# A linear-attention layer in front of a convolution layer: the group norm applied to the turned x on ScalarE, and VectorE's small operations in another order

## What is computed

```python
def _gn(v, G=32, eps=1e-5):            # per image and group of 4 channels
    ...
    return ((g - m) / jnp.sqrt(s + eps)).reshape(v.shape)

# layer 0, on _gn(x): linear attention, 4 heads of 32
q, k, v = split(x @ w_qkv)
q = softmax(q, axis=-2) * scale        # over the 32 numbers of a head
k = softmax(k, axis=-1)                # over the 16384 positions
context = einsum('bhdn,bhen->bhde', k, v)
out = einsum('bhde,bhdn->bhen', context, q) @ w_out + b_out
return layer_norm(out) * g_ln + b_ln
```

## Time and profile before

| | |
|---|---|
| median of 3 runs | 6668.7 us (6665.32 to 6675.22) |
| the profiled execution | 6692.88 us, its span 6691.1 us |
| mean granted clock of TensorE | 0.953 of full speed |
| busy share of the span | PE 86%, DVE 68%, POOL 62%, ACT 54% |

### The profile page before, as it was taken

One profiled execution on the slowest core, in us unless ns is written; L12 is line 12 of the kernel. 1 busy time (PEld: TensorE's weight loads), 2 busy tenths in 40 slices (PEclk: granted clock), 3 DMA queues, 4 the chain that ended last, 5 costly groups with the idle time before them and its releaser, 6 DMA issues. The chain is left out here.

```text
span 6691.1 us, 144257 instructions
## 1 busy us (share of the span) xinstructions
PE 5749.4 (86%) x51796; PEld 5262.7 (79%) x51796; DVE 4552.6 (68%) x5284; ACT 3640.7 (54%) x4872; POOL 4150.8 (62%) x3608
## 2 busy tenths in 40 slices
PE   6789999999999999999995368888888888888887
PEld 5678888888888888888884368788888888787887
DVE  6367777777777777777773786676776666666653
ACT  5555555555555555555541445555555555555554
POOL 0146666666666666666667687677776777676651
PEclk8899999999999999999998689999999999999999
DMA  5356676666766667666656469999999999999987
GB/s 129 125 156 207 201 219 200 206 201 206 214 204 202 200 204 214 204 202 201 198 169 174 130 170 252 251 261 262 263 266 256 255 266 258 255 259 252 262 246 216
DMA packets 1239334, 1441.35 MB, mean 215 GB/s; under 512 B 142960, under 2 KB 1025396, under 8 KB 1238516
## 3 DMA queue, kind: packets, MB, share of 16 engines
q1 hardware_dynamic: 1238516, 1431.07, 75.5%
HBM read 999.09 MB, written 431.64 MB: 214 GB/s over the span
## 5 line engine op out<-in xcount | busy, mean ns | idle before, releaser
L1257 PE MATMUL psC<-wide,xhl 128*128 128x256 bf16 x6144 | 1052.5, 282 | 57.9 <-DMA wide<-toeplitz_wide 40.7
L1254 PE MATMUL psC<-wide,xhl 128*128 128x192 bf16 x6144 | 873.3, 252 | 0.0
L1187 POOL TENSOR_TENSOR stage<-stage,nrow 128x1024 f32<-128x1024 f32 x240 | 612.0, 2550 | 387.5 <-DMA stage<-x_by_block_row 377.8
L1204 POOL COPY down<-xhl 48x448 f32<-48x448 f32 x512 | 516.0, 1008 | 491.7 <-PE psC L1263 387.5
L813 POOL TENSOR_TENSOR y<-y,grow 128x1024 f32<-128x1024 f32 x256 | 603.6, 2358 | 323.7 <-DVE y L657 323.7
L1348 ACT ACTIVATE xhl<-psC 128x512 f32<-128x512 f32 x512 | 303.6, 599 | 694.7 <-PE psC L1263 693.1
L824 POOL TENSOR_TENSOR q<-q,qinv 128x1024 f32<-128x1024 f32 x256 | 489.9, 1914 | 307.4 <-DVE qinv L731 307.4
L1263 PE MATMUL psC<-narrow,down 128*128 128x96 bf16 x6144 | 536.4, 212 | 164.6 <-POOL down L1207 95.2
L657 DVE TENSOR_TENSOR y<-psProj,rstd 128x1024 f32<-128x1024 f32 x256 | 313.6, 1225 | 515.6 <-POOL rstd L805 515.6
L1455 DVE SCALAR_TENSOR_TENSOR xhl<-xhl,psC 128x512 f32<-128x512 f32 x512 | 346.9, 680 | 465.9 <-ACT xhl L1348 465.7
L1254 PEld LDWEIGHTS psC<-wide,xhl 128*128 128x128 bf16 x6144 | 644.6, 116 | 17.6
(11 more groups left out here) (181 smaller groups left out, 14591.1 us busy)
## 6 DMA issues: line engine op xcount, KB each, us to landing
wide<-toeplitz_wide SPq DMA_DIRECT2D x1024, 140.0 KB, 5.9
xa<-in_x SPq DMA_DIRECT2D x256, 512.0 KB, 4.7
xb<-in_x SPq DMA_DIRECT2D x256, 512.0 KB, 3.8
xc<-in_x SPq DMA_DIRECT2D x256, 512.0 KB, 5.7
x_rows<-xc SPq DMA_DIRECT2D x256, 512.0 KB
res<-x_rows SPq DMA_DIRECT2D x256, 512.0 KB, 9.0
out<-res SPq DMA_DIRECT2D x256, 512.0 KB, 8.0
stage<-x_by_block_row SPq DMA_DIRECT2D x225, 512.0 KB, 9.0
```

Of the source, the lines that this page charges most:

```text
L1187: nc.gpsimd.tensor_tensor(v, v, nrow[:, 0:1, :].to_broadcast([P, NP_, C]), ALU.mult).then_inc(s_scaled, 1)
L1204: nc.gpsimd.tensor_copy(dst[lo, :, :, 0:last], src[lo, :, 0:NQ, CW:])
L1254: nc.tensor.matmul(dst[:, :, :, 2:], lhs, tab[:, :, 32 + part * 12:44 + part * 12], start=False, stop=False)
L1257: nc.tensor.matmul(dst, lhs, tab[:, :, part * 16:part * 16 + 16], start=(n == 0), stop=False)
```

## The change

- `wqk`, `shb`, `tq`, `bk`, `ones` and everything that fills them are gone: no scaled weights, no shift matmul (L565), no `split_bias`, no bias matmuls (L514). Keys and queries use `wqkv`.
- ACT normalises `xT[n]` in place: `Identity` with scale and shift from `norm`. Chunk 0 at step 0, behind the copy of `ek` and once `s_norm` is there; each other chunk one step ahead, behind `corr`. PE's `keys` waits for `x_normed`.
- The square of the statistics is now taken from `xT[n-1]` in SBUF, in the next step between the exponential of q and that of k; that of the last chunk follows its copy at once.
- `add_up` of a chunk moves to the next step, right behind `row_sums`; only the last chunk's stays at step 0 before `mean_context`.
- At step 0 `norm_weights` stands ahead of `scale_rows`.
- Small DVE operations on one column (`ksum`, `nmax`, `var`, the shift) become `tensor_scalar` with pointer scalars.

The core of the diff:

```diff
             def keys(img, n, ga, gb):
-                if n == 0:
-                    pe.wait_ge(s_wk, img + 2)
+                pe.wait_ge(x_normed, gb + 1)
                 pe.wait_ge(qt_taken, upto(gb - 1))
                 pe.wait_ge(q_subbed, upto(gb))
-                pe.wait_ge(t_taken, gb + 1)
...
-                for hf in range(2):
-                    nc.tensor.matmul(out[:, hf * 512:(hf + 1) * 512].rearrange("p (t d) -> p t d", d=P),
-                                     ones[:], bk[:].to_broadcast([BK, 4, P]), start=True, stop=False)
-                    for t in range(4 * hf, 4 * hf + 4):
-                        mm = nc.tensor.matmul(out[:, t * P:(t + 1) * P], xT[n][:, t * P:(t + 1) * P],
-                                              wqk[:, 0:C], start=False, stop=(t % 4 == 3))
+                for t in range(TPC):
+                    mm = nc.tensor.matmul(out[:, t * P:(t + 1) * P], xT[n][:, t * P:(t + 1) * P],
+                                          wqkv[:, 0:C], start=True, stop=True)
...
         def _(act):
+            def normalise(n, gb):
+                nc.scalar.activation(xT[n][:], xT[n][:], ACT.Identity, bias=norm[:, 1:2], scale=norm[:, 0:1]
+                                     ).then_inc(x_normed, 1)
+
+            def square(n, count):
+                act.wait_ge(t_taken, count)
+                return nc.scalar.activation(junk[:], xT[n][:], ACT.Square, accum_out=part_sums[:, 1, n:n + 1])
...
+                    if n == 0 and image_live(img + 1):
+                        act.wait_ge(s_norm, img + 2)
+                        act.wait_ge(t_taken, gb + 1)
+                        normalise(n, gb)
+                    if live(img, gb - 1):
                         act.wait_ge(q_subbed, gb)
                         v = q[(n - 1) % 2]
                         nc.scalar.activation(v[:], v[:], ACT.Exp).then_inc(s_qexp, 1)
+                    if live(img, ga - 1) and n:
+                        square(n - 1, ga)
...
+                    if n + 1 < steps and image_live(img + 1):
+                        act.wait_ge(t_taken, gb + 2)
+                        normalise(n + 1, gb + 1)
...
-                        nc.scalar.activation(junk[:], src, ACT.Square, accum_out=part_sums[:, 1, n:n + 1])
-                        nc.scalar.activation(xT[n][:], src, ACT.Identity, accum_out=part_sums[:, 0, n:n + 1]
+                        nc.scalar.activation(xT[n][:], psR[n % 2][:], ACT.Identity, accum_out=part_sums[:, 0, n:n + 1]
                                              ).then_inc(t_taken, 1)
+                        if n == NCH - 1:
+                            square(n, ga + 1).then_inc(s_sq0, 1)
...
-                nc.vector.scalar_tensor_tensor(ksum[:, m + 1:m + 2], ksum[:, m:m + 1], corr[:, m:m + 1],
-                                               ksum_c[:, m:m + 1], ALU.mult, ALU.add)
+                nc.vector.tensor_scalar(ksum[:, m + 1:m + 2], ksum[:, m:m + 1], corr[:, m:m + 1],
+                                        ksum_c[:, m:m + 1], ALU.mult, ALU.add)
...
-                nc.vector.tensor_tensor(nmax[:, n + 1:n + 2], nmax[:, n:n + 1], nmax_c[:, n:n + 1],
-                                        ALU.min).then_inc(s_nmax, 1)
+                nc.vector.tensor_scalar(nmax[:, n + 1:n + 2], nmax_c[:, n:n + 1], nmax[:, n:n + 1], None, ALU.min
+                                        ).then_inc(s_nmax, 1)
...
                     if live(img, gc - 2):
                         row_sums(img, n, gc)
+                    if live(img, gb - 2) and n != 1:
+                        add_up((n - 2) % NCH, gb - 1)
...
+                    if n == 0 and image_live(img + 1):
+                        norm_weights(img, gb)
                     if live(img, gc - 2):
                         scale_rows(n, gc)
...
-                    if n == 0 and image_live(img + 1):
-                        norm_weights(img, gb)
                     if n == 0 and live(img, gb - 1):
-                        add_up(n, gb)
+                        add_up(NCH - 1, gb)
+                    if n == 0 and live(img, gb - 1):
                         mean_context(img, gb)
-                    if n == 0 and image_live(img + 1):
-                        split_bias(img)
                     if live(img, gb):
                         max_k(n, gb)
                     if live(img, gb - 1):
                         sum_q(n, gb)
-                        if n:
-                            add_up(n, gb)
```

More of the change, by code:

```diff
@@ L329, in layer0 @@
         s_pow = sem("b_stat_pow")
[L330 to L334, removed]
+        s_norm = sem("b_norm_ready")
+        x_normed = sem("b_xT_normed")
         k_ready = sem("b_keys")
@@ L362, in layer0 @@
         s_x1 = sem("b_x1")
+        s_sq0 = sem("b_last_squared")
         g_done = sem("b_gram")
@@ L447, in _ @@
             pe.wait_ge(s_const, 16 * NCONST)
-            pe.wait_ge(s_chain, 14)
+            pe.wait_ge(s_chain, 13)
             def buffer(n, turn):
@@ L496, in keys @@
             def keys(img, n, ga, gb):
-                if n == 0:
-                    pe.wait_ge(s_wk, img + 2)
+                pe.wait_ge(x_normed, gb + 1)
                 pe.wait_ge(qt_taken, upto(gb - 1))
                 pe.wait_ge(q_subbed, upto(gb))
-                pe.wait_ge(t_taken, gb + 1)
                 out = buffer(n, 2)
                 for hf in range(2):
-                    mm = nc.tensor.matmul(out[:, hf * 512:(hf + 1) * 512], wqk[:, C:2 * C],
+                    mm = nc.tensor.matmul(out[:, hf * 512:(hf + 1) * 512], wqkv[:, C:2 * C],
                                           xT[n][:, hf * 512:(hf + 1) * 512], start=True, stop=True)
@@ L561, in image @@
                     if live(img, gb):
[L562 to L566, removed]
                         keys(img, n, ga, gb)
@@ L633, in _ @@
             t = Tally(dve, s_chain)
-            t.then(nc.vector.memset(ones[:], 1.0 / 32))
             t.then(nc.vector.memset(acc[:], 0.0))
@@ L658, in scale_rows, with reduce_sums @@
                                         ).then_inc(s_y, 1)
-            def reduce_sums(gb):
+            def reduce_sums(img, gb):
                 dve.wait_ge(t_taken, gb + NCH)
+                dve.wait_ge(s_sq0, img + 2)
                 nc.vector.tensor_reduce(sums1[:], part_sums[:], AX.X, ALU.add).then_inc(s_red, 1)
             def norm_weights(img, gb):
-                base = (img + 1) * 5
+                base = (img + 1) * 4
                 dve.wait_ge(s_stat, img + 2)
@@ L668, in norm_weights @@
                 dve.wait_ge(s_st, base + 1)
-                nc.vector.tensor_tensor(var[:], stat[:, 0:1], stat[:, 0:1], ALU.mult).then_inc(s_st, 1)
+                nc.vector.tensor_scalar(var[:], stat[:, 0:1], stat[:, 0:1], -1.0, ALU.mult, ALU.mult).then_inc(s_st, 1)
                 dve.wait_ge(s_st, base + 2)
-                nc.vector.tensor_tensor(var[:], stat[:, 1:2], var[:], ALU.subtract).then_inc(s_st, 1)
+                nc.vector.tensor_scalar(var[:], var[:], stat[:, 1:2], None, ALU.add).then_inc(s_st, 1)
                 dve.wait_ge(s_st, base + 3)
@@ L674, in norm_weights @@
                 dve.wait_ge(s_pow, img + 2)
[L675 to L704, removed]
-                nc.vector.scalar_tensor_tensor(ksum[:, m + 1:m + 2], ksum[:, m:m + 1], corr[:, m:m + 1],
-                                               ksum_c[:, m:m + 1], ALU.mult, ALU.add)
+                nc.vector.tensor_scalar(norm[:, 1:2], stat[:, 0:1], norm[:, 0:1], -1.0, ALU.mult, ALU.mult
+                                        ).then_inc(s_norm, 1)
@@ L707, in add_up @@
+            def add_up(m, count):
+                dve.wait_ge(ctx_done, count)
+                dve.wait_ge(s_corr, count)
+                dve.wait_ge(acc_done, upto(count - 1))
+                nc.vector.tensor_scalar(ksum[:, m + 1:m + 2], ksum[:, m:m + 1], corr[:, m:m + 1],
+                                        ksum_c[:, m:m + 1], ALU.mult, ALU.add)
                 nc.vector.scalar_tensor_tensor(acc[:], acc[:], corr[:, m:m + 1], psC[:, 0:C],
```

15 lines of the change are left out of this document (3 added, 12 removed).

## The result

The changed kernel takes 6468.3 us, the median of 4 runs (6448.5 to 6477.8), against 6671.4 us for the kernel before: a ratio of 0.9693, 95% interval 0.9668 to 0.9717, 203 us less. The prediction said 205 us less (6464). The profiled execution took 6477.8 us with a span of 6476.0.

What follows compares the result with a forecast made beforehand. PE's work and a ring through DVE were taken as bounds, POOL's ring close behind. 7.8 + 4.0 + 1.4 = 13.2 us an image, 198 in 15, plus 7 for the image before: 205 less, 6464 us; range 6445 to 6485 (0.57).

Steps and rivals of the forecast that it cites:

- The inner step: One chunk step inside an image: from 12.20 to 11.6 us, 0.60 gained in each of 13 intervals, 7.8 an image.
- no wait, but no room either: Before `turn_q` in the inner step: `centre_q` ends 2.7 us behind `project`'s start, `turn_q` could begin at 2.7 to 2.8.
- `add_up` and the minimum: DVE in the inner step: `add_up` (1.09 us) moves into a wait of 2.04; the minimum goes from 0.41 to 0.2.
- The first rival: Small DVE operations stay held by POOL, costing at chunks 0, 1 and 2: 56 us, 6520 in all; chance 0.22.
- The bias matmuls: Two matmuls ahead of the query matmuls on PE: without them 0.44 us less work, PE alone 11.58 us a step.
- two rings of nearly one length: Inner step: PE's own work, 12.0 us, and the ring from keys through DVE's operations and `turn_q` back to keys.
- The slower rival: Normalisation on ScalarE, ahead of `sqo`, becomes the ring: at 5.5 us a piece 56 us slower, 6725; chance 0.02.
- The ring through POOL: `project`, `sqo`, POOL's `q`, `turn_q`: at least 11.5 us; as rival two steps last 23.1 + 0.5, 6503; chance 0.15.
- The end of an image: Boundary from chunk 15 to chunk 0: keys follow context without a wait; sum 3.7 us, taken as 4.0 an image.
- The example of the kernel before: The one image end read for the forecast, B = 1627.17: its step ends at B+22.6, forecast B+18.9.
- more gain: Rival at image ends: PE may keep its full clock, 1.7 us an image, 26 us, 6438; chance 0.04.
- the stop of 3.43 us: Behind the end of chunk 15's `centre_q`: a stop that nothing in the profile releases, forecast to stay.

Runs made afterwards that it cites:

- halved gram: Changed kernel with half of `gram_of` (8 of its 16 matmuls) ahead of `turn_q`: 6400.2 us, ratio 0.9584.
- second power: Changed kernel with a second power on GpSimd in every step, into a spare tile, ahead of `rstd`: 6673.7 us, ratio 0.9989.
- padded kernel: Changed kernel with one more one-column memset on DVE in every step, behind `add_up`: 6467.4 us, ratio 0.9675.
- keys made to wait: Changed kernel with the keys of chunk 0 also waiting for the image's mean context: 6488.4 us, ratio 0.9707.

## Why the prediction was right, point by point

*The total.* That 203 and 205 us lie so close is in part luck. By the traces the first layer became 217 us shorter (the last `centre_q` ends at 3283.1 instead of 3500.4), 12 more than forecast: the ends of images gave more than their terms and the inner steps less. The profiled execution of the kernel before lay 21.5 us above its median and that of the changed kernel 9.5, and this difference takes the 12 us away again.

*The inner step.* Forecast 11.6, measured 11.68. That PE's work would bound it is nearly right: with the bias matmuls back it is 12.12, so each part of a microsecond on PE counts. What I had called "no wait, but no room either" costs 0.15 us or more: `centre_q` can't begin before the queries end (DVE waits 0.58 us for them), and `turn_q` follows its end, so the bound is a ring through PE and DVE of 11.68 us. The halved gram removes it (11.49). The gain was 0.50 us a step where 0.60 was forecast.

*`add_up` and the minimum.* Cost 0 in the new places, as forecast. The trace before could not tell the place from the form. The runs do: undone alone, the place costs 6 us and the form 34, both together 100. The unheld forms take 0.27 (`ksum`) and 0.21 us (`nmax`), near the 0.2 I took; both are covered.

*The first rival* (the small operations stay held) fell. The one-column `tensor_scalar` runs beside POOL, and so does a one-column copy. The Trainium skill, "VectorE: DVE Perf Modes", section "What auto-detection actually checks", gives the two-port mode by the "outermost non-unit dims". The prediction read this as covering a column copied to a column, which has no such dimension beside the partitions; the measurement decides that it isn't covered. For the two-column copy, 1.74 us, the trace agrees with the rule. The price of the rival was put at 56 us. The old forms cost 34 by the medians and 48 in the trace; in 15-0 it is 1.2 us instead of 2.1, as I had given L689's hold in full.

*The bias matmuls.* 0.44 us forecast and measured (12.12 against 11.68). Alone, without DVE's edits, they give 0.22: that two rings of nearly one length must both be shortened was the step of the argument on which the size hung.

*ScalarE.* The normalisation was put at 1.1 us and takes 1.23, the square fits with 0.23 us to spare. The slower rival's room was right: 2.46 us more on ACT make the step 12.0, as its formula gives with 3 x 1.23 us, (23.1 + 0.9) / 2, and the kernel is not slower than before. Its account lacked `ctxg`, which stands behind the normalisation at chunk 0.

*The ring through POOL.* Put at 11.5 us a step and never last. The prediction's first sum for it, 14.18 + 0.1 - 2.82, reads like a ring of one step, by which the second power would have made the step 13.1 us or more. The 12.29 measured shows that it returns over two steps, as the 23.1 us in the rivals have it.

*The end of an image.* Forecast 4.0, measured 6.1; this term was mis-sized. From the keys' start to the end of the step the sum holds: B+11.65 to 18.9 forecast, 7.25 us, and 8.88 to 16.13 measured, also 7.25. What came earlier was context, at B+7.0 to 9.4 instead of 9.85. Most of the 2.1 us beyond the forecast are TensorE's clock, at two places:

- Behind the wait before the keys. The example of the kernel before, 22.6 us, was one of its two shortest image ends in the loop; the mean is 23.54. At nine of the eleven the granted clock fell to half between B+13.8 and B+15.4, about where PE ended its wait for `acc` (2.4 to 4.4 us at the eleven), and work behind it ran slower than in the earlier trace rows, where the keys took 1.94 us. The end 208 us behind the example shows it:

```profile
1849.50 0.71 PE L565 MATMUL psCtx<-wqkv,shb 128*96 128x128 f32 x2 [2.93 <-DVE acc L707]
1850.01 3.19 PE L504 MATMUL psR<-xT,wqk 128*128 128x512 f32 x4
```

In the changed kernel this wait is gone, and the clock doesn't fall there at any end. The mean lies 0.9 us above the example, of which the forecast had allowed 0.3 (for the hold on L722).

- Behind PE's stop at the branch. Gram in the example of the kernel before ran at half clock, 3.38 us from 1631.21 on, and nine of the eleven ends were like it; in the changed kernel six are. At those six the step takes 18.4 us on average, near the 18.9 forecast, at the other five 16.4: 0.9 us in the mean.

In the stretch from 590 to 2900 us of the two traces the granted clock is at half for 75 us before and 20 after. So this was the rival "more gain", with a chance of 0.04 and 26 us (1.7 an image). It came true, and the smaller gain in the inner steps made up for a part of it. Why the clock falls at one end and not at another isn't shown. At the branch it isn't DVE's stop, as the padded kernel too has 20 us. The length of PE's own stop there goes with it only loosely: it is 1.6 to 2.3 us in the changed kernel, 2.3 to 3.0 before and 2.3 to 2.7 with the bias matmuls back, where ten of eleven ends fall; but it also fell behind 1.92 us and not behind 2.30 in one trace. In front of the keys and at chunk 0 to 1 the rows are clearer: nine of eleven ends fell behind waits of 2.4 to 4.4 us (before) and of 2.09 us (old forms), none behind 1.14 us (the keys made to wait) or 0.78 us (the changed kernel).

*The reason given for that term was partly wrong.* I had let the new place of `norm_weights` free the shift of POOL's hold of 2.30 us. The form alone does it: in the old place the shift takes 0.21 us beside POOL's `y`, and the time is the same. And that the stop of 3.43 us stays was wrong; put back by padding it cost 0.3 us an image end.

## What to carry to other kernels

Where two rings are of nearly one length, price an edit by what the second leaves, and look for the edit on the other ring that pays only together with it. An operation held by another engine's has two cures, another place or another form; one is enough, and the form keeps its worth where the schedule slips. Once one engine's own work is the bound, look at its last small wait: other work that is ready, put ahead of the waiting instruction, gave here 68 us for a few moved matmuls. And where a stretch varies from one repetition to the next, read several: the one image end that the forecast went by was 0.9 us shorter than their mean.

## What was unexpected of the hardware

- A one-column copy or `tensor_scalar` between SBUF tensors runs beside a GpSimd `tensor_tensor` (0.15 to 0.27 us), while a two-column copy waits for its end (1.74 us), and so do one-column operations with two SBUF tensors (up to 2.30 us).
- The length of an engine's program in a loop matters: with 16 one-column memsets more per image (191 operations instead of 175) DVE stops for 3.0 to 3.3 us behind the branch, without them it waits 0.36, and that for ScalarE.
- Reading and writing 1024 columns of SBUF in place with scale and bias takes ScalarE 1.23 us, against 1.05 for a square out of SBUF and 1.03 out of PSUM.
- TensorE's granted clock at the image ends was at half (1.2 of 2.4 GHz) for 75 us of 2300 before and for 20 after. Behind PE's stop at the branch very similar rows go either way: 1.92 us of idle time and then gram at 3.47 us, but 2.30 us of idle time and gram at 1.95 at another end of the same trace. About where the waits before the keys end (2.4 to 4.4 us) it fell at nine of eleven ends, and these waits cost more than their own length: the keys behind one took 3.19 us instead of 1.94.
